# A two-layer graph network on one core: windows of 42 nodes, operands moved to PSUM, and the sums of a group turned back by two transposes

## What is computed

```python
# layer 0: attention, 4 heads of 32
xl = (x @ W_lin.T).reshape(N, 4, 32)
alpha = leaky_relu((xl[dst]*att_src).sum(-1) + (xl[src]*att_dst).sum(-1) + (ef*att_edge).sum(-1), 0.2)
e = exp(alpha - segment_max(alpha, dst)[dst])
out = segment_sum(xl[src] * (e / segment_sum(e, dst)[dst])[..., None], dst)
x = layernorm(x + elu(layernorm(out + bias + x) * gamma + beta))
# layer 1: 8 heads of 16, w_ij an edge's 128 numbers, cutoff one number
q, k, v = x @ Wq.T, x @ Wk.T, x @ Wv.T
alpha = (q[dst] * w_ij * k[src]).sum per head / 4 * cutoff
x = layernorm(x + segment_sum(alpha * v[src], dst))
```

## Time and profile before

| | |
|---|---|
| median of 3 runs | 4795.31 us (4794.76 to 4796.04) |
| the profiled execution, its own time | 4802.87 us |
| its span, first to last instruction | 4801.1 us |
| busy: GpSimd | 3583.5 us (75%) |
| busy: VectorE | 2435.6 us (51%) |
| busy: TensorE matmul | 2362.4 us (49%) |
| busy: ScalarE | 588.2 us (12%) |
| DMA, mean over the span | 124 GB/s |
| granted TensorE clock, mean | 0.727 |

### The profile page before, as it was taken

One profiled execution on the slowest core, in us unless ns is written; L12 is line 12 of the kernel. 1 busy time (PEld: TensorE's weight loads), 2 busy tenths in 40 slices (PEclk: granted clock), 3 DMA queues, 4 the chain that ended last, 5 costly groups with the idle time before them and its releaser, 6 DMA issues. The chain is left out here.

```text
span 4801.1 us, 60860 instructions
## 1 busy us (share of the span) xinstructions
PE 2362.4 (49%) x18992; PEld 2166.5 (45%) x18992; DVE 2435.6 (51%) x3629; ACT 588.2 (12%) x893; POOL 3583.5 (75%) x3333
## 2 busy tenths in 40 slices
PE   2333334444444433335556555555555555556654
PEld 2333333333333333334345555555555555555553
DVE  2344444444444444445845555555555555555555
ACT  0111111111111111111420000000000000000002
POOL 5777777777777777773557777777777777777775
PEclk6666666666666666667677878888888787787786
DMA  7433333444444443332344444444444444444443
GB/s 166 104 103 103 100 101 101 109 111 111 111 111 111 107 112 102 101 102 54 107 148 145 142 146 142 146 141 147 143 145 144 143 146 142 146 141 147 141 146 94
DMA packets 324898, 595.82 MB, mean 124 GB/s; under 512 B 101041, under 2 KB 194257, under 8 KB 324593
## 3 DMA queue, kind: packets, MB, share of 16 engines
q0 software_dynamic: 130160, 323.05, 26.5%
q1 hardware_dynamic: 181424, 261.60, 17.1%
q10 hardware_dynamic: 13264, 10.66, 0.7%
HBM read 578.39 MB, written 16.64 MB: 124 GB/s over the span
## 5 line engine op out<-in xcount | busy, mean ns | idle before, releaser
L1157 POOL DMA_INDIRECT ring<-kv_table,den_cols x1616 | 1807.3, 1118 | 518.5 <-issue 518.2
L393 POOL DMA_INDIRECT ring<-x_table,idx x1612 | 1672.7, 1038 | 524.4 <-issue 491.1
L1197 PE MATMUL psum<-ring,work 128*128 128x128 f32 x3232 | 671.6, 393 | 925.0 <-DVE ring L1268 921.3
L1197 PEld LDWEIGHTS psum<-ring,work 128*128 128x128 f32 x3232 | 623.6, 296 | 967.6 <-issue 966.3
L1265 DVE TENSOR_TENSOR ring<-ring 128x1024 f32<-128x1024 f32 x202 | 247.5, 1225 | 871.3 <-POOLq L1169 871.3
L1204 PE MATMUL psum<-work,ring 128*128 128x128 f32 x3232 | 516.1, 327 | 39.7 <-DVE ring L1279 38.8
L1204 PEld LDWEIGHTS psum<-work,ring 128*128 128x128 f32 x3232 | 501.4, 244 | 55.0 <-DVE ring L1279 54.3
L482 PE MATMUL psum<-work 128*128 128x128 f32 x3232 | 490.5, 315 | 14.5 <-DVE work L676 14.5
L1240 ACT ACTIVATE work<-psum 128x1024 f32<-128x1024 f32 x202 | 206.9, 1024 | 2083.8 <-PE psum L1188 2083.8
L482 PEld LDWEIGHTS psum<-work 128*128 128x128 f32 x3232 | 452.6, 224 | 16.2 <-DVE work L676 16.1
L452 PE MATMUL psum<-ident_sb,score 128*128 128x128 f32 x51 | 15.5, 442 | 840.4 <-DVE score L599 840.4
(11 more groups left out here) (161 smaller groups left out, 2218.0 us busy)
## 6 DMA issues: line engine op xcount, KB each, us to landing
dst_all<-dst_row_dram SPq DMA_DIRECT2D x204, 512.0 KB
ring<-ea_dram SPq DMA_DIRECT2D x202, 512.0 KB, 4.0
ring<-kv_table,den_cols POOLq DMA_INDIRECT x1616, 2.9
ring<-x_table,idx POOLq DMA_INDIRECT x1612
ea_pair<-ea_turned_dram SPq DMA_DIRECT2D x102, 128.0 KB, 2.6
ring<-q_table SPq DMA_DIRECT2D x202, 64.0 KB, 1.8
ring<-xpad_dram SPq DMA_DIRECT2D x20, 320.0 KB, 3.4
kv_table<-ring ACTq DMA_DIRECT2D x10, 640.0 KB, 4.1
```

Of the source, the lines that this page charges most:

```text
L393: pool.indirect_dma_start(x_rows[:, h * CHUNK_TILES + t, :], None, k["x_table"], bass.IndirectOffsetOnAxis(idx[h][:, t:t + 1], 0))\
L1157: pool.indirect_dma_start(kv[j][:, t, :], None, k["kv_table"], bass.IndirectOffsetOnAxis(idx[:, tile:tile + 1], 0))\
L1197: last = pe.matmul(q_ps[j % 2][:, t * P:(t + 1) * P], onehotT[:, t * P:(t + 1) * P], q_win[j], start=True, stop=True)
```

## The change

- **Windows of 42 nodes** (`WIN`). One-hots are 128x336. Three bf16 parts of a number now stand as three rows of a window (42 x 3 = 126 rows), so that one product sums the parts: in the scores of layer 0 two matmuls of 512 columns a group take the place of 24, and in layer 1 the q rows are kept as three bf16 parts.
- **Layer 0's sums**: the rows of `x_table` get four ones behind the 128 features, so that the message has 132 columns and carries the denominators. The one-hot is stationary; ScalarE copies the 42x132 result to SBUF, and two transposes turn it back. The splitting of the exponentials and the bf16 copy of the one-hot go.
- **Operands in PSUM**: the node numbers `iota_pass` and the exponentials `ex_ps` in layer 0; `iota_pass`, `alpha` and the first product in layer 1.
- **Layer 1's transposed one-hot** is made by VectorE with a `tensor_scalar` of 126x1024 from `dst_all`, which SyncE loads once a group (512 KB), in place of 8 transposes and ScalarE's copy.
- **Between the layers** GpSimd splits q in three bf16 parts (`split_q`, four instructions of 128x640 a batch), and SyncE stores them.
- In the setup ScalarE copies each pair of node blocks in two instructions (features, attention part) rather than one.
- The scores of layer 0 come out of TensorE turned, and take a copy by ScalarE, 8 transposes and one more copy and addition on VectorE a chunk.

The diff, cut to its core:

```diff
-XROW = FEAT + HEADS0
+MROW = FEAT + HEADS0
+XROW = MROW + HEADS0
 PARTS = 3
+WIN = 42
+KWIN = PARTS * WIN
+PASS_MUL, PASS_SHIFT = 25, 10
+MAX_PASSES = (NODES * PASS_MUL >> PASS_SHIFT) + 1
...
+                    made = pair_ps[j].rearrange("p (b w) -> p b w", b=2)
+                    act.activation(pair[:, :, 0:FEAT], made[:, :, 0:FEAT], ACT.Copy)
+                    act.activation(pair[:, :, MROW:XROW], made[:, :, FEAT:FEAT + HEADS0], ACT.Copy).then_inc(rows_copied, 1)
...
+    iota_pass = k["bank"][3][:, 0:WIN]
+    ex_ps = k["bank"][3][:, P:P + HEADS0 * CHUNK_TILES].rearrange("p (h t) -> p h t", h=HEADS0)
...
             def sums_group(c, g):
                 u = g % 2
                 pe.wait_ge(msg_made, c + g + 1)
                 for t in range(GROUP):
-                    pe.matmul(sum_ps[u], message[u][:, t, :], onehot[u][:, t, :], start=t == 0, stop=t == GROUP - 1)
-                pe.wait_ge(onehot_bf_made, c + g + 1)
...
-                                     onehot_bf[u][:, t, :], start=t == 0, stop=t == GROUP - 1)
-                last.then_inc(summed, 1)
+                    last = pe.matmul(rows_ps[u], onehot[u][:, t, :], message[u][:, t, :], start=t == 0, stop=t == GROUP - 1)
+                last.then_inc(rows_summed, 1)
+
+            def turn_sums(c, g):
+                u = g % 2
+                wait_here(pe, sum_rows_copied, c + g + 1, pe_gate)
+                ident = k["ident_sb"][0:WIN, 0:WIN]
+                pe.transpose(sum_ps[u], sum_rows[u][:, 0:FEAT], ident)
+                pe.transpose(den_ps[u], sum_rows[u][:, FEAT:MROW], ident).then_inc(summed, 1)
...
                     for g in range(CHUNK_GROUPS):
+                        sums_group(c, g)
                         scores_group(d, g)
-                        sums_group(c, g)
+                        turn_sums(c, g)
...
                 for g in range(LAST_GROUPS):
                     sums_group(c, g)
+                    if g:
+                        turn_sums(c, g - 1)
+                turn_sums(c, LAST_GROUPS - 1)
...
-                dve.tensor_tensor(out=onehot[u], in0=k["iota_pass"].unsqueeze(1).to_broadcast([P, GROUP, P]),
+                dve.tensor_tensor(out=onehot[u], in0=iota_pass.unsqueeze(1).to_broadcast([P, GROUP, WIN]),
                                   in1=k["drel"][:, bass.DynSlice(s * CHUNK_TILES + tile, GROUP)].unsqueeze(2)
-                                  .to_broadcast([P, GROUP, P]), op=ALU.is_equal).then_inc(onehot_made, 1)
+                                  .to_broadcast([P, GROUP, WIN]), op=ALU.is_equal)
                 dve.tensor_tensor(
-                    out=message[u].rearrange("p t (h f) -> p t h f", h=HEADS0),
-                    in0=x_rows[:, bass.DynSlice((s % 2) * CHUNK_TILES + tile, GROUP), 0:FEAT]
-                    .rearrange("p t (h f) -> p t h f", h=HEADS0),
-                    in1=ex[:, :, bass.DynSlice(tile, GROUP)].rearrange("p h t -> p t h").unsqueeze(3)
-                    .to_broadcast([P, GROUP, HEADS0, FEAT // HEADS0]),
+                    out=message[u].rearrange("p t (f h) -> p t f h", h=HEADS0),
+                    in0=x_rows[:, bass.DynSlice((s % 2) * CHUNK_TILES + tile, GROUP), 0:MROW]
+                    .rearrange("p t (f h) -> p t f h", h=HEADS0),
+                    in1=ex_ps[:, :, bass.DynSlice(tile, GROUP)].rearrange("p h t -> p t h").unsqueeze(2)
+                    .to_broadcast([P, GROUP, MROW // HEADS0, HEADS0]),
                     op=ALU.mult).then_inc(msg_made, 1)
 
...
+            def split_q(u, n):
+                q = qkv[u][:, :, 0:FEAT]
+                pool.wait_ge(qkv_copied, BATCH * (n + 1) + 2)
+                if n > 1:
+                    pool.wait_ge(q_out[u], 16 * (n // 2))
+                pool.tensor_copy(q_parts[u][:, :, 0, :], q)
+                for p in range(1, PARTS):
+                    pool.drain()
+                    last = pool.tensor_tensor(out=q if p < PARTS - 1 else q_parts[u][:, :, p, :], in0=q, in1=q_parts[u][:, :, p - 1, :],
+                                              op=ALU.subtract)
+                    if p < PARTS - 1:
+                        pool.drain()
+                        pool.tensor_copy(q_parts[u][:, :, p, :], q)
...
+                if n:
+                    split_q(1 - u, n - 1)
             first_power(BATCHES - 1)
             second_power(0, BATCHES - 2)
+            split_q(1, BATCHES - 3)
             second_power(1, BATCHES - 1)
+            split_q(0, BATCHES - 2)
+            split_q(1, BATCHES - 1)
...
+    iota_pass = k["bank"][1][:, 0:WIN]
     message = [tiles3(part(GP)) for _ in range(2)]
     idx = k["idx1"]
-    alpha = part(GROUP * HEADS1)
+    alpha = k["bank"][1][:, P:P + GROUP * HEADS1]
...
+                    sp.wait_ge(onehotT_made, n0 + j + 1)
+                    sp.dma_start(dst_all[j % 2], k["dst_row"][0:1, bass.DynSlice((SLOTS * i + j) * GP, GP)]
+                                 .to_broadcast([P, GP])).then_inc(dst_in[j % 2], 16)
                     sp.wait_ge(msg_made, n0 + j + 1)
-                    sp.dma_start(q_win[j], k["q_table"][bass.DynSlice(starts[j], P), :]).then_inc(q_in[j], 16)
+                    sp.dma_start(q_win[j], k["q_table"][bass.DynSlice(starts[j], WIN), :, :].rearrange("n s f -> (n s) f"))\
+                      .then_inc(q_in[j], 16)
...
-            def make_onehot(i, j):
-                dve.tensor_tensor(out=onehot[j], in0=k["iota_pass"].unsqueeze(1).to_broadcast([P, GROUP, P]),
+            def make_onehot(i, n, j):
+                dve.wait_ge(dst_in[j % 2], 8 * n + 16 - 8 * (j % 2))
+                dve.wait_ge(q_spread, n + 1)
+                dve.tensor_scalar(onehotT[j % 2], dst_all[j % 2][0:KWIN, :], k["base_f"][0:KWIN, bass.DynSlice(i, 1)],
+                                  k["node_pass"][0:KWIN, :], ALU.subtract, ALU.is_equal).then_inc(onehotT_made, 1)
+                dve.tensor_tensor(out=onehot[j], in0=iota_pass.unsqueeze(1).to_broadcast([P, GROUP, WIN]),
                                   in1=k["drel"][:, bass.DynSlice(i * GROUP, GROUP)].unsqueeze(2)
-                                  .to_broadcast([P, GROUP, P]), op=ALU.is_equal).then_inc(onehot_made, 1)
+                                  .to_broadcast([P, GROUP, WIN]), op=ALU.is_equal)
 
             def messages(i, n, j, nth):
+                dve.wait_ge(kv_ready, n + 1)
+                dve.wait_ge(q_spread, n + 3)
+                q = tiles3(q_ps[j % 2])
+                dve.tensor_tensor(out=q, in0=q, in1=kv[j][:, :, 0:FEAT], op=ALU.mult)
+                dve.drain()
                 dve.wait_ge(w_in[j], 16 * (nth + 1))
-                dve.wait_ge(kv_ready, n + 1)
-                dve.tensor_tensor(out=prod, in0=kv[j][:, :, 0:FEAT], in1=w[j], op=ALU.mult)
-                dve.drain()
-                dve.wait_ge(q_spread, n + 2)
-                dve.tensor_tensor(out=prod, in0=prod, in1=tiles3(q_ps[j % 2]), op=ALU.mult).then_inc(q_used, 1)
```

More of the change, by code:

```diff
@@ L517, in _, with copy_dst_scores, exponentials @@
         def _(act):
-            passes = act.value_load(k["passes_sb"][0:1, 0:1], min_val=1, max_val=NODE_BLOCKS)
-            group = counter(act, "act_group0")
-            def chunk(s, groups):
+            def copy_dst_scores(s):
+                act.wait_ge(scores_summed, s + 1)
+                act.activation(dst_scores, dst_ps, ACT.Copy).then_inc(dst_copied, 1)
+            def exponentials(s):
                 act.wait_ge(shifted, s + 1)
```

351 lines of the change are left out of this document (188 added, 163 removed).

## The result

| | before | the change |
|---|---|---|
| median of 4 runs each, same chip | 4795.03 us (4793.86 to 4796.04) | 4503.11 us (4499.09 to 4503.79) |
| the profiled execution, its own time | 4802.87 | 4502.56 |
| its span | 4801.1 | 4500.8 |

The ratio is 0.939 (95% interval 0.9373 to 0.9406): 292 us less, where 265 was forecast. The forecast was 4530, its range 4440 to 4640. The times of these seven say nothing of the 4503, so only their gathers' durations are read. Four of them were run again with the same kernels (r1, r2, r7, r8); e6, e10 and e11 were not.

The account below looks back on a forecast made before the run. GpSimd's issue of gathers was taken as the bound in both layers. Terms -97 - 238 + 56 + 10 + 4 = -265 us from 4795.3 gave 4530 us; range 4440 to 4640, 8 in 10.

Parts of the forecast that it names:

- a product holds a gather wherever its inputs lie: Rival for both layers: gathers keep their times despite operands in PSUM, giving 4907 us; chance 4%.
- the two signs of being wrong: GpSimd waiting for landings, or gathers above 1.2 us that no tensor_scalar or scan touches.
- Part 1: Operands to PSUM: the layers' loops could lose 158 and 280 us; after added costs layer 0 gets -97.
- The floor of 1.25 us a gather: Gather period with VectorE idle, 945 ns plus 0.305 us before each: 2015 us for layer 0, 2020 for layer 1.
- Part 2: Layer 1's new transposed one-hots hold gathers 0.21 us each, 42 us in all (0 to 95); layer 1 -238.
- Part 3: SyncE's load of target numbers in layer 1 costs 0, with an upper end of 60 us.
- 3 us of delay are covered: Layer 1: gathers land after 2.9 us, GpSimd's wait comes 5.95 us after the start, so later landings cost nothing.
- the new load delays landings: Rival in layer 1: GpSimd waits for landings past 5.95 us; one us beyond costs 202 us, giving 4732; chance 5%.
- Part 4: Between the layers, GpSimd's split of the queries costs +56 us (ends +40 and +85).
- The circle: Between the layers, ScalarE's work, GpSimd's split and power, and the way back: 18.6 us a batch, 6.2 more, eight times.
- Part 5: Layer 0's last chunk: VectorE's addition waits behind the next group's products, 1 us a group, +10 (0 to +25).
- Part 6: Setup: ScalarE's second small copy instruction for each of 25 pairs costs +4 us (0 to +10).

Follow-up runs that it names:

- these seven: The seven of the twelve experiments in whose runs the kernel before itself took 6097 to 6141 us.
- r1: Rerun of the kernel before with only its operands moved to PSUM (windows of 128 kept): 4416.75 us against 4801.38, ratio 0.9202.
- r2: Rerun of the change with its operands back in SBUF and keys times weights first: 4966.31 us, ratio 1.035.
- r7: Rerun of the change with queries split one batch later, last chunk's groups turned at once, arrivals awaited behind the sixth gather: 4445.64 us, ratio 0.926.
- r8: Rerun of the change with layer 1's load of target numbers cut to one row (4 KB instead of 512 KB a group): 4499.77 us, ratio 0.9374.
- e6: The change with GpSimd asking for a group's arrival behind the next group's sixth gather instead of fourth: 5963.39 us, ratio 0.9763.
- e10: The change with r7's three repairs and transposed one-hots made by comparing with a PSUM column instead of by tensor_scalar: 5873.97 us against 6097.35.
- e11: The change's layer 0 with last-chunk repair and e10's comparison, joined to r1's kernel between the layers and in layer 1: 6155.03 us against 6097.35.

## Why the prediction was right

The forecast case came true: the place of the operands decides (rival "a product holds a gather wherever its inputs lie": excluded by r1 and r2 together, 0.9202 and 1.035). The mechanism was right, and the sizes of its small terms were not; by parts they miss by 1 to 19 us, mostly to the same side. One of the two signs of being wrong did appear, GpSimd's waits for landings. By its parts:

- **Part 1, -97 for layer 0; -116 measured.** The floor of 1.25 us a gather held. Of the 61 us that were added back, 35 came, and with them 9 us that the sum left out, of longer gaps behind the fifth gather of a chunk, before as after. The scans and the rest of `maxima` cost 17.7 us, where 18 was taken. The one-hots cost 17.0 us, where 43 was taken: 0.08 us each, not 0.21. The twelve of the earlier trace rows were too few to stand for the phases of 204.
- **Part 2, 42 us for layer 1's new one-hots; 23.5 measured**, 0.12 each. Without the landing waits, in r8, it is 43.0, or 0.21 each.
- **Part 3, 0 for the new load; 17 measured.** "3 us of delay are covered" failed twice. The delay was larger where it counts: the eighth gather of a group, the last that GpSimd waits for, landed 2.9 us after its start in the median before, 4.5 at most, and lands after 5.0 now, 6.3 at most (of the 134 whose landing is in the trace). And the cover was smaller than 5.95 us: in no group does the next gather start less than 0.89 us after the last landing, while without a wait it starts 0.30 us after the gather before it. So a landing later than 5.95 + 0.30 - 0.89 = 5.36 us already makes GpSimd wait; 47 of the eighth gathers are later than that, 5 later than 5.95. In r8 the latest is 5.33, and there is no wait. The rival "the new load delays landings" came true at a twelfth of its price.
- **Parts 2 and 3 together** give -239 where -238 was forecast. That is luck, two errors that cancel; r8 shows that they are coupled: take the load away, and the layer keeps its length.
- **Part 4, +56; +39 measured.** The circle was the right one, sized too long: in it, GpSimd's split of the batch before waits 4.5 to 5.6 us for ScalarE, and then takes 4.6. The rows that answer to the earlier trace rows:

```profile
2231.81 0.72 POOL L911 CAST ring<-ring 128x640 bf16<-128x640 f32 x1 [5.57 <-ACT ring L1023]
2232.67 1.39 POOL L914 TENSOR_TENSOR ring<-ring 128x640 f32<-128x640 f32 x1
2234.20 0.72 POOL L918 CAST ring<-ring 128x640 bf16<-128x640 f32 x1
2235.05 1.39 POOL L914 TENSOR_TENSOR ring<-ring 128x640 bf16<-128x640 f32 x1
2236.41 1.18 POOL L898 TENSOR_TENSOR ring<-ring 128x5 f32<-128x5 f32 x1
...
2248.27 0.72 POOL L911 CAST ring<-ring 128x640 bf16<-128x640 f32 x1 [4.50 <-ACT ring L1023]
```

  A cast takes 0.72 us (taken: 1.0), a subtraction 1.39 (1.5), which makes the split 0.9 shorter; ScalarE's part takes 9.1 to 9.6 (9.7) and the way from L902 to its start 1.6 (2.2). The period is 16.5 to 17.0 us where 18.6 was counted. r7, with the split one batch later, has 13.5 to 13.7 at last and is 29 of the 39 us shorter: the circle was the cause of these.
- **Part 5, +10; +18 measured, within its ends.** The sum took 2.2 us for the products of a group; they took 3.2 to 3.75, at a granted clock of 0.60 in this stretch, where the kernel before had 0.78. With the order of r7, at 0.94, they take 2.0, and 27 us are to be had there.
- **Part 6, +4; -3 measured**, between executions that differ by as much (r1, with the old setup, 47.6; r2, r7 and r8, with the new, 44.7 to 45.0).

The profile's slight bias helped too: the execution of before lay 8 us above its median, the one of after at it, so the spans differ by 300 and the medians by 292.

## What to carry to other kernels

Where GpSimd's descriptor work bounds a kernel, look at what the gathers run beside before touching their number: moving one input of each large VectorE product to PSUM gave 384 us here, almost alone (r1), and the other edits of the change together cost some 86 on top. Test a bundle of edits by its parts, in both directions: the change was worth 0.939, its first part 0.920, and the rest without that part 1.035. When a circle of three engines sets a period, ask of each added step which neighbour's wait it stands behind; put it one turn later if it has the slack.

## What the runs showed of the hardware

- **The hold works both ways.** The `tensor_scalar` takes 0.81 us, and 0.96 at 3007.14, where it starts 0.51 us into a gather; in the mean it takes 0.86 in layer 0, where r2 has 0.81. By the Trainium skill (SBUF — State Buffer, Who interferes with whom) an instruction of VectorE in a two-port mode and one of GpSimd exclude each other, and whichever comes second is blocked for the whole instruction. The trace agrees in that either can be held, and differs in how long. A gather that a one-hot holds ends 0.80 to 0.83 us after the one-hot, as behind a product; the one-hot that a gather holds takes at most 1.05 us, so 0.24 more. And in layer 1 of the change no gather that starts up to 0.144 us into a one-hot is held, while every one that starts from 0.145 us on is.
- **An operand in PSUM can be faster in itself.** The same product of 128x1056 with an operand whose innermost stride is 384 bytes takes 1.24 us from PSUM and 1.95 from SBUF (L717 in the change and in r2).
- **SyncE can be slow by itself.** In e6 its own instructions for the load of w (L1212), against those of the change, from 3600 to 4100 us (minimum, median and maximum in ns):

```profile
L1212 SPq FUSED_REGOPS  x38: 15/582/1395, 3610.6 to 4096.7; - x38
...
L1212 SPq DMA_DIRECT2D ring<-ea_dram x38: 5/690/710, 3610.7 to 4098.0; - x38
```

```profile
L1212 SPq FUSED_REGOPS  x49: 37/37/37, 3605.9 to 4093.2; - x49
...
L1212 SPq DMA_DIRECT2D ring<-ea_dram x49: 352/352/358, 3606.0 to 4093.3; - x49
```

  The same kernels were then 640 (r2's) to 1890 us (r1's) slower, and the order of the versions changed: r1's kernel, 8% faster than before otherwise, came out 3% slower. Those of the other engines kept their durations: in e10 an unheld gather took 0.95 us and a product of 1024 columns 1.22. The cause was not found, and that the slow instructions make the whole difference was not shown; a median without a kernel to compare on the same chip would have misled.
